# A six-layer decoder on one core: spare products and the norm's place in the state-space layer, and the order of sums, norms and one addition in three attention layers

## The reference, cut to what matters

```python
# 1 state-space layer
h = h * exp(dt * A) + x_t * (dt * B_t)        # 256 channels x 16 states, a scan over 128 tokens
y = sum(h * C_t) + x * D;  y = y * silu(z);  out = y @ W_out + b_out
# 2 two attentions (self, then over the context), 16 heads of 32, each with an MLP
a = softmax(q @ k^T * 32 ** -0.5);  a = a * mask (self only);  x = x + (a @ v) @ li1 + b;  x = x + mlp(norm(x))
# 3 channel mix
# 4 gated linear attention, 16 heads of 8
O1 = cumulative products of q with k * v;  E = v - shifted O1;  O2 = the same with other keys on E
out = (O1 + O2) @ c_proj^T
# 5 narrow cross attention, 16 heads of 8      # 6 eight experts, one for each token
```

## Time and profile before

| | us |
|---|---|
| median of three runs | 3566.37 |
| the profiled execution: time | 3561.62 |
| the profiled execution: span | 3559.8 |
| state-space phase (0 to 845) | 845 |
| self attention (845 to 1480) | 635 |
| cross attention (1650 to 2165) | 515 |
| gated phase (2415 to 2900) | 485 |

### The profile page before, as it was taken

How to read it: one execution, slowest core, us unless ns; L and a number is a source line. 1 busy time by engine, 2 the same in 40 slices (tenths; PEclk the granted TensorE clock), 3 DMA queues, 4 the chain that set the end, 5 groups by cost and what they waited for, 6 DMA issues and landing times. The chain is left out here.

```text
span 3559.8 us, 101883 instructions
## 1 busy us (share of the span) xinstructions
PE 3143.7 (88%) x41041; PEld 1946.3 (55%) x41041; DVE 2404.4 (68%) x5635; ACT 1981.7 (56%) x3574; POOL 2062.4 (58%) x1842
## 2 busy tenths in 40 slices
PE   6888788877899999898999998999999989999676
PEld 3433343333555555565666666675555545656575
DVE  5998999985555555485556555876777765666465
ACT  5666666663566666442555554335666646666354
POOL 5888888884678787663111113546777752433365
PEclk8999999988999999998999999999999989999798
DMA  4222222224700000000000000000000000000364
GB/s 145 98 88 90 91 91 88 90 87 160 259 2 2 2 2 2 16 1 12 5 5 5 5 2 6 1 8 8 2 2 2 2 17 17 27 16 15 94 173 118
DMA packets 50328, 165.43 MB, mean 46 GB/s; under 512 B 11822, under 2 KB 23217, under 8 KB 40784
## 3 DMA queue, kind: packets, MB, share of 16 engines
q1 hardware_dynamic: 45520, 150.43, 12.9%
q0 software_dynamic: 4352, 8.47, 0.7%
HBM read 149.89 MB, written 43.65 MB: 54 GB/s over the span
## 5 line engine op out<-in xcount | busy, mean ns | idle before, releaser
L529 DVE TENSOR_TENSOR_SCAN XC<-ssm_dA,ssm_db 128x2048 f32<-128x2048 f32 x128 | 565.2, 4415 | 69.8 <-PE ssm_db L374 59.9
L478 ACT ACTIVATE ssm_dA<-ssm_delta,ssm_nega 128x508 f32<-128x508 f32 x512 | 325.7, 707 | 139.4 <-DVE XC L529 136.2
L1219 POOL TENSOR_TENSOR self_pm<-self_pT,weights 128x512 f32<-128x512 f32 x256 | 322.7, 1294 | 61.7 <-ACT self_pT L948 60.2
L593 POOL TENSOR_TENSOR XC<-XC,XB 128x1536 f32<-128x1536 f32 x64 | 253.3, 3958 | 92.6 <-DVE XC L529 92.6
L374 PE MATMUL ssm_db<-XB,ssm_dxT 32*128 32x128 f32 x4096 | 166.8, 305 | 144.6 <-DVE XC L529 135.5
L1225 POOL TENSOR_TENSOR XC<-XC,XB 128x128 f32<-128x128 f32 x128 | 58.5, 457 | 400.5 <-DVE XB L1102 400.5
L593 POOL TENSOR_TENSOR ssm_hC<-XC,XB 128x1536 f32<-128x1536 f32 x64 | 256.2, 4003 | 54.7 <-DVE XC L529 54.6
L374 PEld LDWEIGHTS ssm_db<-XB,ssm_dxT 32*128 32x128 f32 x4096 | 140.0, 204 | 235.2 <-DVE XC L529 214.5
L1088 DVE TENSOR_REDUCE self_nmax<-self_scores 128x4 f32<-128x512 f32 x256 | 158.4, 681 | 87.2 <-PE self_scores L828 87.1
L2654 POOL TENSOR_TENSOR XC<-XC,weights 128x512 f32<-128x512 f32 x128 | 161.6, 1283 | 95.8 <-ACT XC L2488 95.8
L2662 POOL TENSOR_TENSOR XC<-XC,weights 128x512 f32<-128x512 f32 x128 | 161.3, 1281 | 34.5 <-ACT XC L2497 34.3
(11 more groups left out here) (456 smaller groups left out, 8375.6 us busy)
## 6 DMA issues: line engine op xcount, KB each, us to landing
XB<-c_rows SPq DMA_DIRECT2D x64, 1024.0 KB
sorted<-in_padding SPq DMA_DIRECT2D x1, 33280.0 KB, 109.0
experts_we<-in_w_experts SPq DMA_DIRECT2D x72, 323.0 KB, 3.5
experts_rt<-sorted SPq DMA_DIRECT2D x72, 65.0 KB
ssm_xT<-in_xT SPq DMA_DIRECT2D x16, 256.0 KB
XC<-in_w_experts SPq DMA_DIRECT2D x9, 256.0 KB
weights<-in_w_self SPq DMA_DIRECT2D x1, 1412.0 KB, 7.3
cross_ctx_t<-in_ctx SPq DMA_DIRECT2D x16, 77.0 KB
```

What stands on the lines that cost most here:

```text
L478: o = act.activation(dA[:, p % 2, :].rearrange("p (b k t) -> p b k t", b=GROUP, k=4)[:, :, k, 1:T], by_batch(delta[:, slot, half, :])[:, : ...
L529: dve.tensor_tensor_scan(states(p).rearrange("p m t -> p (m t)"), dA[:, p % 2, :], db[:, :], 0.0, ALU.mult, ALU.add).then_inc(h_ready, 1)
L593: pool.tensor_tensor(weighted(p).rearrange("p (b k) t -> p b k t", k=4)[:, :, 0:3, :], states(p).rearrange("p (b k) t -> p b k t", k=4)[:, ...
L1219: pool.tensor_tensor(pm[:, n % 2, r, :].rearrange("p (h t) -> p h t", h=4), pT[:, n % 2, r, :].rearrange("p (h t) -> p h t", h=4), bcast(V ...
```

## The change

State-space: TensorE makes the two unread products at p = 6 as well, behind the transposes, and waits there for ScalarE's two reads. GpSimd does the part of `diag` first and the norm's four steps behind it, at p = 5 in place of p = 6. Self: at beats with t % 4 = 0 the sums of t-3 come behind the first scores of t+1. Cross: `ctx_norm` moves to the end of VectorE's beat. Gated: ScalarE's copy of O2 goes; VectorE adds O2 (in PSUM) to o1T at the start of the step, and TensorE makes one product of the sum in place of two accumulated ones.

```diff
@@ ssm, TensorE
                         head(g + 1, 1 - slot, p)
-                        if p == 7:
-                            pe.wait_ge(proj_read, (g + 2) * N_ACT)
+                        if p >= 6:
+                            if p == 6:
+                                pe.wait_ge(proj_read, (g + 2) * N_ACT)
                             for j in range(2):
                                 pe.matmul(pj[j][:, :], ident, dxT[:, 1 - slot, j, :, :].rearrange("p c d -> p (c d)"))
@@ ssm, GpSimd
-                    if p == 6 and there(g - 1):
+                    if there(g) and more(g):
+                        head(g + 1, 1 - slot, p)
+                    if p == 5 and there(g - 1):
                         pool.wait_ge(vec, g * VEC)
...
                         pool.tensor_scalar(shift[:, :], shift[:, :], -1.0, None, ALU.mult).then_inc(pool_step, 1)
-                    if there(g) and more(g):
-                        head(g + 1, 1 - slot, p)
@@ wide attention, TensorE
+        SUMS_BEHIND = (0,) if own else ()
...
-                if there(t - 3):
+                behind = t % GROUP in SUMS_BEHIND
+                if there(t - 3) and not behind:
                     sums(t - 3)
                 if there(t + 1):
                     first_scores(t + 1)
+                if there(t - 3) and behind:
+                    sums(t - 3)
@@ wide attention, VectorE
                     if not own and p == 3:
                         row_norm(g)
-                        ctx_norm(g)
+
+            def late_norms(t):
+                g, p = t // GROUP + 2, t % GROUP
+                if not own and g < NG and p == 3:
+                    ctx_norm(g)
...
                 for g, n in late_jobs(t):
                     empty(g, n)
+                late_norms(t)
@@ gated, TensorE
-                        pe.wait_ge(o2_ready, n + 1)
-                        pe.matmul(acc[b % 2][:, 2 * T:2 * T + C], o1T[:, b % 2, :], wo, start=True, stop=False)
-                        pe.matmul(acc[b % 2][:, 2 * T:2 * T + C], o2T[:, :], wo, start=False, stop=True).then_inc(out_mm, 1)
+                        pe.wait_ge(o12_ready, n + 1)
+                        pe.matmul(acc[b % 2][:, 2 * T:2 * T + C], o12T[:, :], wo).then_inc(out_mm, 1)
@@ gated, ScalarE
-                    if now := lagged(g, p, 2, slot):
-                        n, _, b, s = now
-                        act.wait_ge(av2_mm, n + 1)
-                        if needed(n):
-                            act.wait_ge(out_mm, n)
-                        act.activation(o2T[:, :], acc[b % 2][:, 3 * T:4 * T], ACT.Identity).then_inc(o2_ready, 1)
@@ gated, VectorE
                 for p in range(GROUP):
+                    if now := lagged(g, p, 3, slot):
+                        n, _, b, s = now
+                        dve.wait_ge(av2_mm, n + 1)
+                        if needed(n):
+                            dve.wait_ge(out_mm, n)
+                        dve.tensor_tensor(o12T[:, :], acc[b % 2][:, 3 * T:4 * T], o1T[:, b % 2, :], ALU.add).then_inc(o12_ready, 1)
```

More of the change, by code:

```diff
@@ L2258, in linear_attention_phase @@
         o1T = ph.sb("o1T", [P, 2, T])
-        o2T = ph.sb("o2T", [P, T])
+        o12T = ph.sb("o12T", [P, T])
         y = ph.sb("y", [P, 2, GROUP, C])
@@ L2268, in linear_attention_phase @@
         (power_set, setup, zeroed, fold_mm, folded, qn_ready, vp_ready, proj_mm, by_act, by_dve, s1_mm, s2_mm, m1_dve, m1_act,
-         m1_pool, m2_dve, m2_act, m2_pool, av1_mm, o1_ready, e_mm, e_ready, av2_mm, o2_ready, out_mm, out_read, vec,
+         m1_pool, m2_dve, m2_act, m2_pool, av1_mm, o1_ready, e_mm, e_ready, av2_mm, o12_ready, out_mm, out_read, vec,
          pool_step, x_out) = (ph.sem(n) for n in (
@@ L2272, in linear_attention_phase @@
              "s2_mm", "m1_dve", "m1_act", "m1_pool", "m2_dve", "m2_act", "m2_pool", "av1_mm", "o1_ready", "e_mm",
-             "e_ready", "av2_mm", "o2_ready", "out_mm", "out_read", "vec", "pool_step", "x_out"))
+             "e_ready", "av2_mm", "o12_ready", "out_mm", "out_read", "vec", "pool_step", "x_out"))
         mark = ph.sem("mark")
```

## The result

The changed kernel takes 3518.7 us (median of four runs, 3512.9 to 3520.38) where the kernel before takes 3566.5; the ratio is 0.9864, with a 95% interval of 0.985 to 0.9878. That is 48 us less. The profiled execution took 3520.38 us with a span of 3518.5, 41 us less than that of before, which was a low one of its kernel's runs as this one is a high one. So 7 of the 14 us that I missed are that choice of runs, and 7 are in the trace.

What follows compares the result with a forecast made beforehand. VectorE's scans were taken to bound the state-space phase, TensorE the two wide attentions and the gated phase. Terms -21 - 3 - 11 + 1 = -34 us gave a forecast of 3532 against the median, range 3518 to 3550.

Steps and rivals of the forecast that it cites:

- State-space: State-space phase: diag ahead of the norm and two more unread products save 1.5 us at 14 boundaries, -21 us.
- Self: Self attention: sums behind the first scores end VectorE's 0.20 us wait in 15 beats, -3 us; bounds 0 and -5.
- Cross: Cross attention, p = 3: late ctx_norm ends a 0.78 us TensorE stall 14 times, -11 us; bounds -11 and 0.
- Gated: Gated phase: four step changes sum to +0.1 us a period, +1 us over 15 periods; bounds -15 and +18.
- the case that I had put among the bounds: State-space: unread products end late, so L374 of p = 7 and its scan slip up to 1.98 us; +28 us, unlikely.
- two things side by side: State-space: GpSimd's earlier diag saves 1.5 us a boundary; the two more products cost nothing and keep TensorE's clock up.
- The slower rival: State-space: GpSimd's product of p = 7 gets in ahead of waiting L535; +3.3 us at 14 boundaries, 3578; chance 0.04.
- the meeting that was to decide: State-space: scan of p = 7 ends (near 481.8) before diag (482.15), so L535 meets GpSimd at every boundary.
- At p = 0 ScalarE was last, and is relieved: -0.25: Gated phase, step p = 0: without its copy and wait ScalarE is relieved, making the step 0.25 us shorter.
- The changes of p = 2 and p = 3: Gated phase: VectorE's addition lengthens step p = 2 by 0.4 us and p = 3 by 0.33 us.
- That the period would stay within 0.3 us of its length: Gated phase, a sign of being right: the four-step period changes by no more than 0.3 us.
- the bound of the gated phase (-15): Gated phase: VectorE pays the addition in no step and TensorE's 0.23 us comes home in 64, -15 us.

Runs made afterwards that it cites:

- the part alone: Kernel before with only one part of the change applied: ratio to before 0.9944 for the state-space edits, 0.9969 for the late ctx_norm in cross.
- The attempt above: Changed kernel with VectorE's four gated norm instructions (L141) moved from the end of p = 1 to p = 0: ratio to before 0.9985, 43 us over the changed kernel.

## Why the prediction was right or wrong

**State-space: right in its mechanism, and in its number partly by luck.** -21 against -21.6 in the trace and -20 for the part alone. The unread products ended 0.24 us ahead of the scan (0.2 forecast), the clock held, the interval was 11.67 for 11.9: GpSimd's product of p = 6 took 3.54 and not 4.06, since VectorE's L536 no longer runs beside its start. Over the 14 boundaries that gives 1.69 us each, -23.7, where I had 1.5. The boundary of group 0 gave 1.9 us of it back: the case that I had put among the bounds, products that end late, did come there, and I had counted that boundary at nothing. The two nearly cancel. What I treated as two things side by side, too, hang on one another; the products by themselves cost 12 us.

**The slower rival did not come.** GpSimd's last part of `diag` ended at 421.97 and the scan at 421.82, so the meeting that was to decide took place for 0.15 us. L536 took its 0.69 and did not wait; GpSimd's next product waited instead, with 4.04 us where it takes 3.54 alone, and so at all 14 boundaries. A longer meeting, though, stood in the trace of before, and the prediction made no use of it. At nine of its boundaries the scan of p = 7 ended inside the last part of `diag`, as here (VectorE, then GpSimd):

```profile
182.25 1.27 DVE L535 TENSOR_TENSOR ssm_hC<-XC,XB 128x512 f32<-128x512 f32 x1
```
```profile
181.90 1.07 POOL L573 TENSOR_TENSOR XB<-ssm_Bt,weights 128x512 f32<-128x512 f32 x1
182.92 4.00 POOL L593 TENSOR_TENSOR ssm_hC<-XC,XB 128x1536 f32<-128x1536 f32 x1
```

L535 waited for `diag` (1.26 to 1.44 us for 0.69) and each time got in ahead of the product, which then took some 4.0. So the rows of before already excluded this rival, at nine meetings and not at one. The attempt above shows the same in another place: L141, with one SBUF input, stretched from 1.10 to 4.06 us beside GpSimd's masks, and L2546 from 0.21 to 1.34. L2546 has two SBUF inputs, and so has L535, which took 1.35 us in the earlier trace rows where it takes 0.69 alone: it started at 469.04, while GpSimd was in the instruction ahead of its product of 469.81. Whether the number of inputs has a part in it no run here shows; L141 was stretched with one.

**Cross: right.** 0.78 forecast, 0.79 measured at each p = 3, 11 us by the part alone. `ctx_norm` is covered by VectorE's idle time at p = 0.

**Self: right by the period.** 0.33 in place of 0.20 a period: TensorE's stall at L852 shrank from 0.68 to 0.40, and some 0.05 came elsewhere; 4 us for 3. The rest of the 10 us between the two profiles was scatter.

**Gated: wrong.** The step that failed is "At p = 0 ScalarE was last, and is relieved: -0.25". It was -0.71, and the run with ScalarE's wait and copy kept shows that all of it is ScalarE's release. The prediction gives no row for its 0.25. I had carried the 0.33 us that TensorE loses at p = 3 over to VectorE as well and put its masks of p = 0 behind that. But VectorE lost almost nothing there: before, its statistics ended 1.54 us after the step's first scores had started, after 0.97, because the scores came 0.31 later and a pause of 0.22 in the statistics was gone. These are VectorE before and after around the start of that step (first scores at 2654.46 and at 2610.56):

```profile
2655.68 0.32 DVE L128 BATCH_NORM_AGGREGATE gla_mv<-gla_stats 128x2 f32<-128x6 f32 x3 [0.22 <-issue]
2655.91 0.66 DVE L2585 TENSOR_TENSOR XC<-gla_scores,weights 128x512 f32<-128x512 f32 x1
```
```profile
2611.15 0.38 DVE L128 BATCH_NORM_AGGREGATE gla_mv<-gla_stats 128x2 f32<-128x6 f32 x4
2611.45 0.26 DVE L2587 TENSOR_TENSOR gla_o12T<-gla_out,gla_o1T 128x128 f32<-128x128 f32 x1
2611.77 0.69 DVE L2594 TENSOR_TENSOR XC<-gla_scores,weights 128x512 f32<-128x512 f32 x1
```

The masks now start as the scores end, and so does ScalarE's half. With the measured value the sum for the phase is -0.43 x 15 = -6.5 us in place of +1. The changes of p = 2 and p = 3 were right to 0.03. That the period would stay within 0.3 us of its length was wrong.

**The total.** With -6.5 for gated and -4 for self the sum is -43 against the medians' -48. The remaining 5 us are within what the intervals leave (0.985 to 0.9878 is 10 us wide). The other kernels' profiles show where they may lie. Phase by phase, the mean over the profiles in which a phase has its old code, less the mean over those in which it has the code of the change, is 24.6 us for state-space (844.8 in four, 820.2 in six), 4.2 for self, 10.8 for cross (535.2 and 524.4) and 7.6 for gated (497.4 and 489.8): 47 in all. So most of the 5 us are in the state-space phase, whose old form varied from 841.3 to 849.5 us and stood at its shortest in the profile of before. The boundaries account for 21.8 of the 24.6; where the rest comes from stays open. All four parts came out within their own bounds; the range was too narrow at its lower end because it took the bound of the gated phase (-15) into no case of its own.

## What to carry to other kernels

The 0.33 us that TensorE lost at p = 3 of the gated phase did not shift VectorE: carry a delay on only to those engines that truly wait, and give the rest the time as slack, or a step that is relieved comes out too small. Look at the wait that follows unread products before adding them: here the clock held at 1.00 where that wait was 0.91 us, but in front of one of 2.71 us they moved the idling, and the slow clock (a mean of 0.68), behind them, and cost 12 us. Check their margin at the first group as well: there ScalarE's reads ended 0.04 us ahead of the scan, and some 2 us ahead in the later groups. And take the mean of a step apart before calling it unchanged: one short instruction of VectorE that sometimes meets GpSimd (L2546, 0.21 or 1.34 us) made two lengths of it here, 8.40 and 9.07 us. And VectorE's idle time at p = 0 of the gated phase, 1.65 us, was no free place for its four norm instructions: beside GpSimd's masks they took 4.06 us in place of 1.10.

## What was unexpected of the hardware

A wait cost TensorE much more than its length: in the gated phase, which ran at a mean clock of 1.00 before the change and 0.99 after it, a wait of 1.70 us was followed by a fall of the clock, to a mean of 0.53 over 3.35 us, and by L2370 at 2.09 us in place of 1.14, the step went from 6.77 to a median of 10.5, and the four-step period from 29.0 to 31.9. A VectorE instruction of 0.21 us (L2546) took 1.34 where it had to wait for a GpSimd mask (1.27), and with that alone the step with p = 2 was 0.47 to 0.67 us longer. And phases that nobody touched differ by up to 10 us from one profile to another (narrow attention, 426.0 to 436.5), more than two of the four parts of this change bring. A single pair of profiles can't price a part of 4 us, the period inside the phase can.
